# Reciprocals by quarters and a rewritten epilogue in a split-precision attention layer

## What is computed

```python
qkv = einsum('bchw,oc->bohw', x, w_qkv)          # x (16, 512, 32, 32)
sim = einsum('bhdi,bhdj->bhij', q * SCALE, k)    # 8 heads, n = 1024
attn = softmax(sim, axis=-1)
out = einsum('bhij,bhdj->bhid', attn, v)
y = einsum('bchw,oc->bohw', out, w_out) + b_out
mean_sq = mean(y * y, axis=1, keepdims=True)
y = y * rsqrt(mean_sq + SCALE) * rms_scale
return y + x
```

## Time and profile before

| | us |
|---|---|
| median of 3 runs | 3982.03 (3979.09 to 3989.03) |
| profiled execution | 3985.51 |
| its span, first to last instruction | 3983.7 |
| tensor engine busy | 3914.2 (98%) |
| GpSimd busy | 2979.6 (75%) |
| vector engine busy | 2787.3 (70%) |
| scalar engine busy | 2310.8 (58%) |

### The profile page before, as it was taken

One profiled execution on the slowest core, in us unless ns is written; L12 is line 12 of the kernel. 1 busy time (PEld: TensorE's weight loads), 2 busy tenths in 40 slices (PEclk: granted clock), 3 DMA queues, 4 the chain that ended last, 5 costly groups with the idle time before them and its releaser, 6 DMA issues. The chain is left out here.

```text
span 3983.7 us, 53076 instructions
## 1 busy us (share of the span) xinstructions
PE 3914.2 (98%) x18624; PEld 2458.8 (62%) x18624; DVE 2787.3 (70%) x2834; ACT 2310.8 (58%) x4044; POOL 2979.6 (75%) x2340
## 2 busy tenths in 40 slices
PE   8999999999999999999999999999999999999996
PEld 6666666666666666666666666666666666666662
DVE  6667676677766767677676766767667676677764
ACT  4556565565655656565565555655656565565653
POOL 5678777786876778777787777877778777786875
PEclk9999999999999999999999999999999999999997
DMA  4111111111211211102011111111111111110100
GB/s 149 50 46 54 43 64 54 43 60 36 69 48 43 74 32 63 55 35 72 32 64 54 38 69 54 43 53 53 62 46 54 43 65 53 43 62 34 69 17 32
DMA packets 71271, 212.18 MB, mean 53 GB/s; under 512 B 8152, under 2 KB 8280, under 8 KB 58208
## 3 DMA queue, kind: packets, MB, share of 16 engines
q1 hardware_dynamic: 71008, 208.80, 14.8%
HBM read 168.92 MB, written 39.85 MB: 52 GB/s over the span
## 5 line engine op out<-in xcount | busy, mean ns | idle before, releaser
L1138 POOL TENSOR_TENSOR prob_sum<-prob_sum,probs 128x512 f32<-128x512 f32 x1536 | 1964.1, 1308 | 335.2 <-ACT probs L771 335.2
L771 ACT ACTIVATE probs<-score 128x512 f32<-128x512 f32 x2048 | 1110.2, 595 | 771.7 <-PE score L677 765.4
L980 DVE TENSOR_REDUCE maxima<-aux 128x1 fp32r<-128x1024 f32 x768 | 913.6, 1217 | 441.0 <-PE aux L653 264.8
L690 PE MATMUL pv<-probs,v_sb 128*64 128x512 f32 x4096 | 994.6, 607 | 0.0
L668 PE MATMUL score<-q_hl,k_hh 128*128 128x512 f32 x2048 | 841.6, 411 | 10.6 <-ACT probs L771 10.6
L677 PE MATMUL score<-q_hm,k_l 72*128 72x512 f32 x2048 | 814.8, 398 | 0.5 <-DVE q_hm L998 0.5
L517 PE MATMUL aux<-x_hi,w_ring 128*128 128x512 f32 x2048 | 656.6, 397 | 9.8 <-DMA scale_sb<-scale 8.9
L1134 POOL TENSOR_TENSOR prob_sum<-probs 128x512 f32<-128x512 f32 x256 | 327.6, 1300 | 391.8 <-ACT probs L771 389.6
L690 PEld LDWEIGHTS pv<-probs,v_sb 128*64 128x64 f32 x4096 | 249.2, 136 | 481.7 <-issue 474.1
L668 PEld LDWEIGHTS score<-q_hl,k_hh 128*128 128x128 f32 x2048 | 387.5, 189 | 179.7 <-issue 86.4
L517 PEld LDWEIGHTS aux<-x_hi,w_ring 128*128 128x128 f32 x2048 | 387.8, 189 | 97.0 <-DMA scale_sb<-scale 8.9
(11 more groups left out here) (93 smaller groups left out, 5108.7 us busy)
## 6 DMA issues: line engine op xcount, KB each, us to landing
w_ring<-w_split SPq DMA_DIRECT2D x93, 1024.0 KB, 4.8
stage<-x SPq DMA_DIRECT2D x256, 256.0 KB, 4.7
out<-stage SPq DMA_DIRECT2D x128, 256.0 KB, 2.0
w_split<-w_ring SPq DMA_DIRECT2D x3, 1024.0 KB, 12.6
w_split<-y_sb SPq DMA_DIRECT2D x3, 1024.0 KB, 3.9
y_sb<-wqkv SPq DMA_DIRECT2D x4, 512.0 KB, 8.3
probs<-wqkv SPq DMA_DIRECT2D x2, 512.0 KB, 7.1
probs<-wout SPq DMA_DIRECT2D x1, 1024.0 KB, 8.3
```

The source lines that it names most:

```text
L690: pe.matmul(pv[half][e * D:(e + 1) * D, :], v_sb[:, pair // 2, j, (pair % 2) * P + e * D:(pair % 2) * P + (e + 1) * D], probs[:, (b * SLOT ...
L771: act.activation(probs[:, step % RING, e, :], score[e][:], ACT.Exp, scale=SOFT).then_inc(prob_ready, 1)
L980: dve.tensor_reduce(maxima[:, n:n + 1], bank(k, 2), AX_X, ALU.max).then_inc(aux_free[k], 1)
L1138: pool.tensor_tensor(prob_sum[:, e, :], prob_sum[:, e, :], probs[:, step % RING, e, :], ALU.add).then_inc(prob_added, 1)
```

## The change

In the loop, the reciprocal of the mean squares is made in four quarters of 128 columns instead of two halves of 256: at places 10, 12, 14 of the slot and 0 of the next one. The root waits for all four.

In the last slot of the last batch, O0 and O1 run at t = 9, after value steps 0 and 1; the copy to the high part moves from t = 4 to 6, and the low part goes from GpSimd to the vector engine. All four squares of half 0 follow at t = 9. The vector engine adds them, and R of half 0 comes at t = 13 behind value steps 4 and 5, which move there from the epilogue. In the epilogue the reciprocal of the sums reads PSUM directly. The scalar engine multiplies y by the scale of the channel; GpSimd multiplies half 0 by the root and adds the residual. R of half 1 is four matmuls on the four squares, accumulated, in place of three additions and one matmul. Its root, multiplication, residual and store go by column halves on scalar engine, vector engine and SyncE, for all four rows at once, from `last_rows`, which lies in the then unused half of v_sb and is loaded before the first half's stores.

```diff
-INVERT_AT = (((0, 10), (0, 12)), ((1, 10), (1, 12)))
+INVERT_AT = (((0, 10), (0, 12), (0, 14), (1, 0)), ((1, 10), (1, 12), (1, 14), (2, 0)))
+LAST_HIGH_AT = 6
+LAST_OUTPUT_AT = 9
...
-    if t == 11 and preceding:
+    if t == (11 if following else LAST_OUTPUT_AT) and preceding:
...
-    if t == 13 and preceding:
+    if t == (13 if following else LAST_OUTPUT_AT) and preceding:
...
+        last_rows = v_sb[:, 0].rearrange("p (m j) n -> p m (j n)", j=2)
...
-            for half in range(2):
-                load_resid(B - 1, half)
-                store_half(B - 1, half)
+            load_resid(B - 1, 0)
...
             for m in range(MT):
-                sp.wait_ge(out_stored[m], 16 * 2 * B)
+                sp.dma_start(last_rows[:, m, :], x_v[B - 1, m, :, HALF:N]).then_inc(last_rows_loaded, 16)
+            store_half(B - 1, 0)
+            for part in range(2):
+                cols = slice(part * HALF // 2, (part + 1) * HALF // 2)
+                sp.wait_ge(last_rows_added, part + 1)
+                for m in range(MT):
+                    sp.dma_start(out_v[B - 1, m, :, HALF + part * HALF // 2:HALF + (part + 1) * HALF // 2],
+                                 last_rows[:, m, cols]).then_inc(out_stored[m], 16)
...
-                        pe.wait_ge(sq_added, 3 * (2 * batch + half + 1))
-                        pe.matmul(bank(k), ones_c[:].bitcast(F32), sq_a[:], start=True, stop=True
-                                  ).then_inc(aux_full[k], 1)
...
+                        if name == "R0":
+                            pe.wait_ge(sq_added, 3 * (2 * batch + half + 1))
+                        parts = squares[:1] if name == "R0" else squares
+                        for m, part in enumerate(parts):
+                            if name == "R1":
+                                pe.wait_ge(sq_made, 4 * (2 * batch + half) + m + 1)
+                            last = pe.matmul(bank(k), ones_c[:].bitcast(F32), part[:],
+                                             start=(m == 0), stop=(m == len(parts) - 1))
+                        last.then_inc(aux_full[k], 1)
...
+                            if t == 13 and body.last and slot == SLOTS - 1:
+                                values(body, slot, 4, False)
+                                values(body, slot, 5, False)
+                                item(Body(epi, B - 1, False, True), 0, "R0")
...
-                act.wait_ge(inv_ms_ready, 2 * (done + 1))
+                act.wait_ge(inv_ms_ready, 4 * (done + 1))
...
+            act.activation(table_back[:], ones_d[:, 0:1], ACT.Sqrt)
+            act.wait_ge(inv_ms_ready, 4 * (2 * (B - 1) + 1))
+            act.activation(rms_a[:], rms_b[:], ACT.Sqrt).then_inc(rinv_ready, 1)
+            for m in range(MT):
+                act.wait_ge(sq_made, 4 * 2 * (B - 1) + m + 1)
+                act.activation(y_sb[:, 0, m, :], y_sb[:, 0, m, :], ACT.Identity, scale=scale_sb[:, m:m + 1]
+                               ).then_inc(y_prescaled, 1)
...
-                cols = slice(part * HALF // 2, (part + 1) * HALF // 2)
+                cols = slice(part * HALF // 4, (part + 1) * HALF // 4)
                 dve.reciprocal(rms_b[:, cols], rms_a[:, cols]).then_inc(inv_ms_ready, 1)
...
+            dve.wait_ge(sums_ready, B * SLOTS)
             for part in range(2):
-                invert_sums(end, 0, part)
+                cols = slice(part * HALF // 2, (part + 1) * HALF // 2)
+                dve.reciprocal(inv_sum[:, cols], pv[0][:, cols]).then_inc(inv_ready, 1)
             normalise(end, 0)
-            for m in range(MT):
-                scale_y(end, 0, m)
+            split_output_low(dve, B * SLOTS)
...
+                y = y_sb[:, 1, :, cols]
+                dve.wait_ge(rinv_ready, 2 * (B - 1) + 1 + part + 1)
+                dve.tensor_tensor(y, y, rms_a[:, cols].unsqueeze(1).to_broadcast([P, MT, HALF // 2]), ALU.mult
+                                  ).then_inc(y_scaled, 1)
...
+                dve.tensor_tensor(last_rows[:, :, cols], last_rows[:, :, cols], y, ALU.add
+                                  ).then_inc(last_rows_added, 1)
```

More of the change, by code:

```diff
@@ L348, in split_output_low, with output_high_at, low_by_gpsimd, add_squares @@
                               ).then_inc(olo_ready, 1)
+        def output_high_at(body, slot):
+            return LAST_HIGH_AT if body.last and slot == SLOTS - 1 else OUTPUT_HIGH_AT[slot]
+        def low_by_gpsimd(body, slot):
+            return not (body.last and slot == SLOTS - 1)
+        def add_squares(eng, done):
+            for m in range(1, MT):
+                eng.wait_ge(sq_made, 4 * done + m + 1)
+                if m > 1:
+                    eng.wait_ge(sq_added, 3 * done + m - 1)
+                eng.tensor_tensor(sq_a[:], sq_a[:], squares[m][:], ALU.add).then_inc(sq_added, 1)
         def run_bodies(eng, one):
@@ L721, in one @@
                                     maxima_of_tile(body, slot, 2)
+                                if j == 2 and "O0" in names:
+                                    item(body, slot, "O0")
+                                    item(body, slot, "O1")
                                 values(body, slot, j, False)
@@ L751, in _ @@
             last = Body(epi, B - 1, False, True)
-            for j in range(STEPS // 2, STEPS):
+            for j in range(STEPS - 2, STEPS):
                 values(end, SLOTS - 1, j, True)
-            item(last, 0, "R0")
             sums(end, 0)
@@ L840, in split_output_high, with square @@
                 act.activation(o_hi[:], o_norm[:], ACT.Copy).then_inc(ohi_ready, 1)
-            def square(body, half, m):
-                batch = body.b if SQUARE_AT[half][m][0] == 7 and body.plan is not epi else body.b - 1
+            def square(body, half, m, own=False):
+                batch = body.b if own else body.b - 1
                 done = 2 * batch + half
@@ L898, in one @@
                             for m in range(MT):
-                                if (slot, t) == SQUARE_AT[half][m] and (slot == 7 or not body.first):
-                                    square(body, half, m)
+                                own = SQUARE_AT[half][m][0] == SLOTS - 1
+                                if (slot, t) == SQUARE_AT[half][m] and not (body.last if own else body.first):
+                                    square(body, half, m, own)
+                        if (slot, t) == (SLOTS - 1, LAST_OUTPUT_AT) and body.last:
+                            for m in range(MT):
+                                square(body, 0, m, True)
                         if t == 0 and not (body.last and slot == SLOTS - 1):
@@ L946, in _ @@
                 square(end, 1, m)
-            root(2 * (B - 1) + 1)
+            for m in range(MT):
+                act.wait_ge(sq_made, 4 * (2 * (B - 1) + 1) + m + 1)
+                act.activation(y_sb[:, 1, m, :], y_sb[:, 1, m, :], ACT.Identity, scale=scale_sb[:, m:m + 1]
+                               ).then_inc(y_prescaled, 1)
+            for part in range(2):
+                cols = slice(part * HALF // 2, (part + 1) * HALF // 2)
+                act.wait_ge(inv_ms_ready, 4 * (2 * (B - 1) + 1) + 2 * (part + 1))
+                act.activation(rms_a[:, cols], rms_b[:, cols], ACT.Sqrt).then_inc(rinv_ready, 1)
         @block.vector
@@ L1079, in one @@
                                     scale_y(body, half, m)
+                        if t == output_high_at(body, slot) and not low_by_gpsimd(body, slot):
+                            split_output_low(dve, body.b * SLOTS + slot)
                         if (slot, t) in SPLIT_LOW_AT and not body.last:
@@ L1139, in add_probs @@
                                            ALU.add).then_inc(prob_added, 1)
-            def add_squares(done):
-                for m in range(1, MT):
-                    pool.wait_ge(sq_made, 4 * done + m + 1)
-                    if m > 1:
-                        pool.wait_ge(sq_added, 3 * done + m - 1)
-                    pool.tensor_tensor(sq_a[:], sq_a[:], squares[m][:], ALU.add).then_inc(sq_added, 1)
             def split_squares_low(done):
@@ L1174, in one @@
                     for j in range(STEPS):
-                        if j == OUTPUT_LOW_AT and not (body.first and slot == 0):
+                        if j == OUTPUT_LOW_AT and low_by_gpsimd(body, slot) and not (body.first and slot == 0):
                             split_output_low(pool, body.b * SLOTS + slot)
```

56 lines of the change are left out of this document (31 added, 25 removed).

## The result

| | us |
|---|---|
| changed kernel, median of 12 runs | 3978.03 (3955.91 to 3986.43) |
| kernel before, median of 12 runs beside them | 3989.11 (3977.97 to 4006.51) |
| ratio after to before | 0.9969, 95% interval 0.9955 to 0.9983 |
| profiled execution of the changed kernel, its span | 3978.09, 3976.0 |

So the change gains, but 11 us of the 25 forecast (10.8 and 13.9), and the time lies 9 us above the range. The kernel before stands 7 us above the three runs from which the forecast started. The 12 times are not a cloud. They read 3955.9, 3963.8, 3971.7, 3973.1, then eight between 3977.6 and 3986.4: steps of about 8 us on top of 3956.

What follows compares the result with a forecast made beforehand. The tensor engine was taken to set the pace, with waits between engines in the tail. Profiled 3985.5 less 10.8 (loop) and 13.9 (tail) gave 3960.8; from the runs' mean 3958.7, so forecast 3959 us, range 3951 to 3969.

Steps and rivals of the forecast that it cites:

- Part 1, T's wait: Slot 0: transpose T no longer waits for the vector engine's second output addition; 0.72 us a batch, 10.8 us gained.
- the third quarter: Slot 0, vector engine: this quarter reciprocal ends 0.4 us before the mask products of T are due.
- its gap: Vector engine ahead of slot 1's maxima: 1.38 us idle, of which the fourth quarter fills 0.95.
- The rival of slow quarters: Loop reciprocals: a quarter takes as long as a half, 29.9 us lost less the tail's 13.9, 4001.5; chance 0.03.
- Part 2, the tail: Last slot and epilogue: reordered work shortens the span from 3983.7 to 3969.8, 13.9 us gained; bounds 7.8 and 16.5.
- wait ahead of the sums: End of the last slot: GpSimd's probability additions end it at 3940.2 (3939 to 3942); sums start then, not at 3946.66.
- the R matmuls: Epilogue: four matmuls on the squares, 1.0 us each at 2.4 GHz, the fourth taken to end at 3956.4.
- The rival of the low clock: Epilogue: R matmuls run at the low clock throughout, 3.9 us later, 3963; chance 0.13.
- Nothing in the change moves the two against each other, as both follow from T: Slot 1: first scaling of y and a GpSimd subtraction start together; who loses stays unchanged on average, -7 to +8 us.
- a lost collision: Slot 1: when the vector engine's scaling loses to GpSimd, the slot is longer by about 1.0 us in all.
- the coin's 7 us: Slot 1: scaling against GpSimd, lost in 7 of 15 batches; up to 7 us gain, taken as zero on average.
- the other rivals: Low clock 3963, chance 0.13; all slot 1 collisions lost 3967, 0.09; no loop gain, T waiting otherwise, 3969.8, 0.07.

Runs made afterwards that it cites:

- the kernel with one input: Changed kernel, the vector engine's scaling in the loop multiplying by a constant, with one SBUF operand instead of two: 3954.92 us, ratio 0.9901 to the kernel before.
- the kernels that were to force it: Changed kernel with row 2's second-half residual at step 2 instead of 4: 3958.98 us; the same plus GpSimd's one-column write: 3960.15 us.
- the one with 120 columns: Changed kernel with a 120-column memset on the vector engine ahead of the scaling at (2, 4): 3955.65 us, ratio 0.9933 to the kernel before.
- the one with one column: Changed kernel with a one-column memset on the vector engine ahead of the scaling at (2, 4): 3959.84 us, ratio 0.9913 to the kernel before.
- the residual at step 2: Changed kernel with GpSimd's residual of row 2, second half, at step 2 of slot 2 instead of 4: 3958.98 us on the second chip, ratio 0.9938.

## Why the prediction was wrong

**Part 1, T's wait: right.** 15 waits are gone, slots 0 are shorter by 0.64 and slots 1 by another 0.10; 15 x 0.74 = 11.1 for 10.8. A quarter takes 0.94 or 0.95 for 0.95, the third quarter left 0.42 for 0.4, and the fourth fit in its gap. The rival of slow quarters is out.

**Part 2, the tail: right, 14.2 us for 13.9.** The changed kernel's last T is 6.46 us later in its trace than before's (3918.99 against 3912.53). With that taken off, step by step:

| end of | forecast | measured |
|---|---|---|
| wait ahead of the sums | 3940.2 | 3940.5 |
| reciprocals of the sums | 3944.5 | 3945.0 |
| low part | 3947.4 | 3948.1 |
| second output addition | 3953.5 | 3954.0 |
| R | 3956.4 | 3956.9 |
| last quarter | 3960.6 | 3961.1 |
| last addition | 3965.7 | 3965.8 |
| span | 3969.8 | 3969.6 |

The low part took 1.66 beside GpSimd, for 1.5, and the R matmuls ran at a granted clock of 1.00, as taken. From the sums to the last quarter each end lies 0.3 to 0.7 late; the two multiplications, two additions and the stores then gave back 0.7, so a part of the close fit is luck. The rival of the low clock is out.

**The step that failed: "Nothing in the change moves the two against each other, as both follow from T".** It was said of the one meeting that I had found, in slot 1, and it was wrong twice. First, in slot 1 the change did move them: GpSimd's subtraction now starts 182 to 195 ns behind the scaling (46 to 55 before), and the vector engine won all 15 in the profile, 7.1 us that I had put only into the range. Second, and worse, the paragraph took slot 1 for the only place where nanoseconds decide. Of the same instruction there are four more in slots 1 and 2. At (2, 4) it stood 140 to 159 ns behind a GpSimd start, and I added a quarter at (2, 0) without asking what it does to that distance. Nothing of it was left but some 10 ns to either side: the meeting cost three stalls of 8 us, 24.3 us, in the profiled execution.

**The price was wrong too.** For a lost collision I took 1.1 us, the most that the trace of before shows (1.89 for 0.75). It can be 6.1 us of the instruction and 8 us of the kernel. No row of before has that. Without the three of the profiled execution its time is 3978.1 - 24.3 = 3953.8. The prediction's sum for the profiled execution, with the coin's 7 us won, was 3960.8 - 7 = 3953.8 as well. The lowest single times of the changed kernel, 3955.9 beside the result and 3953.7 on the second chip of the experiments, lie there too (on the fourth it was 3961.3). So the sum of the parts held, and one thing was left out of it. (The rival of slow quarters was added up from 3985.5, the other rivals from the forecast of 3959, so its 4001.5 stands 2 us too high beside them.)

**Who gets the ports.** The Trainium skill, "SBUF: State Buffer" (section on the two separate sides), says that whichever of the two starts first has the pair for its whole instruction, while the other fully blocks. By that rule the scaling here would wait for one GpSimd instruction at most, some 1.25 us, as it does in most batches (1.84 for 0.75). The traces don't bear this out for a shut-out: six GpSimd instructions ran one after another, each in its usual time, while the vector engine stood waiting. On who wins, the rule also fails here by the start times of the trace: the scaling started 3 and 6 ns first and lost for 7.97, and in slot 1 of the kernel before it started 46 to 55 ns first and lost 7 of 15. The same page of the Trainium skill has operations with one SBUF input contend when they run in a two-port mode; the kernel with one input would agree, 0.49 where it starts first and 1.27 in the median, though no view shows in which mode it ran.

**What is shown and what is not.** Shown: the quarters alone bring the loop's gain; the new tail brings its own; each slot of 38 us in a profile holds one scaling of 8 us and no other instruction above 1.8; without the quarters of half 1 the distance is back, none of the 75 scalings at such a distance was shut out, and the nine runs of the version without it lie within 3.4 us on two chips. Not shown: why at the same distance one batch is shut out and the next isn't, and why the same program stands a few ns otherwise on different chips (GpSimd behind at (2, 4) in 11, 9 and none of 15 batches of the changed kernel). That a shut-out ends when GpSimd stops is read from 16 of them; the kernels that were to force it had none at (2, 4). Single runs a step above the rest also came from kernels whose own profile has no long slot: the one with 120 columns, the one with one input, the one with one column and the changed kernel on the second chip. What those executions held is not on record.

The kernel before and the kernel with halves in the loop spread most of all, up to 4012 and 4003, more than 15 collisions of 1 us can give, and no profile tells why. On the fourth chip the kernel before also lies in groups some 8 us apart, 3979 to 3983, 3987 to 3989 and 3995 to 3996, and its mean granted clock is 0.994 in the first and 0.992 in the others. A shut-out with its 6.8 us at 0.50 would lower that mean by an estimated 0.0009 (3.4 of 3976). So shut-outs in the kernel before are a rival that stands untested; the place would be slot 1, where GpSimd starts 46 to 55 ns behind the scaling, next to the 36 and 43 ns at which two were shut out at (2, 4). The changed kernel moved that meeting to 163 ns and more on every chip. If so, a part of its gain comes from there.

## What to carry to other kernels

Before an instruction is added on one of two engines that share a port, list every place where the other starts within some 120 ns of it (the widest distance of a shut-out here was 119), with its distance, what the added instruction does to that distance, and what is queued behind the loser up to the tensor engine. The price of such a meeting isn't the usual one in the trace but can be the time until the other engine has to stop by itself (here 3.0 us where it had two instructions to go, 8.0 where it had six). Where a kernel's single times come in even steps, look in a profile, slot by slot, for the one that is longer by that step; and make only the half of a change that pays, here the quarters of half 0.

## What the hardware showed that I had not expected

- A vector instruction that reads two SBUF operands can be held for 7.9 to 8.0 us while GpSimd's instructions follow each other without a gap; 8 of 225 at (2, 4), seven of them with GpSimd starting 3 to 43 ns behind.
- It ends 0.55 us after GpSimd's last instruction, 16 times of 16. At (2, 10), where GpSimd stops after two instructions, the same hold lasts 3.0 to 3.2 us and costs the slot some 0.2: two in the changed kernel on the second chip, one on the fourth, three with the 120 columns, one with the one column, one with the residual at step 2 on the second chip.
- One more vector instruction in the queue made a later one start 0.115 us earlier.
- A wait of 5.95 us of the tensor engine cost 2 more, at a granted clock of 0.50 for the 6.8 us after it.
- A write of one column on the vector engine (0.06 us) between two instructions delays the next by at most some 5 ns, one of 120 columns by 0.11 us.
- A reciprocal of 128 columns takes 0.94 or 0.95, one of 256 takes 1.75 by the earlier trace rows.
